# An MoE block on one core: tokens sorted by expert instead of by pair of experts, in tiles of 512 rows that are stored split in 16 bit and loaded transposed

## The chip, the cores and the metric

The kernel runs on one core of a Trainium2 chip. The metric is the device time of one execution, in microseconds (us). Five engines run side by side and meet through semaphores: TensorE (PE in the profile; PEld is its weight load), VectorE (DVE), ScalarE (ACT), GpSimd (POOL) and SyncE (SP). DMAs are issued from SP, ACT and POOL, and all of them run on the core's 16 DMA engines.

## The reference

The input x is 32 images of 128 channels and 32 x 32 pixels, f32. What is computed:

```
u  = layernorm over channels (x)
wt = (max(u) @ w2.T + b2) - (mean(u) @ w1.T + b1)    # 9 taps for each image and channel, softmax over the taps
x1 = x + u + depthwise_3x3(u, wt) + bias             # still image by image
t  = x1 as 32768 tokens of 128 features
q  = layernorm over features (t)
g  = q @ Wg + bg                                     # 8 logits; the two largest, softmax over those two
out = t + sum over the two chosen experts e of w_e * (gelu(q @ W1[e] + b1[e]) @ W2[e] + b2[e])   # 128 -> 512 -> 128
```

The products of the experts are made in f16 with the operands split in a high and a low half (high x high + low x high + high x low), at three times the work of one product.

## The kernel before, in words

There are three stages, one after the other. The order of the work is written out by hand for each engine; an engine does its list in that order and waits on semaphores.

**The conv stage** (`run_steps`) handles two images (16 blocks of 128 tokens) per step, in a pipeline of four sub-stages: layer norm and taps, convolution, turning into tokens with the statistics (`turn`, `token_std`, `keep`), and routing (`choose`, `ranks`, `place`, `weigh`). Each step of the loop thus does a part of four different pairs of images; there are 16 pairs. Routing finds for each token which of the 28 unordered pairs of experts it goes to, and its place in the list of this pair. GpSimd then writes the rows of a pair of images to DRAM with indirect DMAs, one for each block of 128 tokens, so 16 a step (line 439); the index of each row is computed on DVE. One row is 133 f32: the raw token, two weights, the token's number and two numbers with which ACT normalises it later. `rows` has two buffers: ACT's `keep` waits for the DMAs of the pair before the last (`rows_out`), and so does DVE's `place` for `idx`. After the last pair DVE makes a table of the tiles from the counts (lines 1087 to 1123), and SP and ACT write padding rows behind the end of each list (`pad`).

**The tile stage** runs over NT = 32768/256 + 28 = 156 tiles of 256 tokens, each with one pair of experts (`dstep` on PE, ACT and DVE, the loop of lines 442 to 454 on POOL). SP loads a tile's rows from DRAM into one of RING = 6 buffers as soon as the output of the tile six before has left (`y_out`). ACT normalises, PE transposes, ACT and DVE split the result in f16 halves. For each of the two experts PE does the up product (`up`: 12 matmuls of 256 columns), ACT the gelu, ACT or DVE the split of the hidden values, PE the down product (`down`: for each of 4 quarters of the hidden layer and 2 blocks of tokens one matmul of 256 columns against the weights' both halves and one of 128 columns; then the bias). DVE weighs and adds the two experts' results (`combine`), POOL adds the halves and the token itself (lines 447, 449) and writes the two blocks to their places in DRAM with an indirect DMA each (line 454).

**The final stage** loads each image's tokens (512 KB) from DRAM, PE turns them back to channels, DVE copies them from PSUM, and ACT issues the store of the image.

## Time and profile before

| | |
|---|---|
| median of 3 runs | 1804.54 us (1803.85 to 1805.2) |
| span of the profiled execution | 1798.2 us |
| own time of the profiled execution | not given apart; its span lies 6.3 us below the median of the runs |
| PE busy | 1536.5 us (85%) |
| DVE busy | 1396.4 us (78%) |
| ACT busy | 1202.0 us (67%) |
| POOL busy | 866.1 us (48%) |
| moved by DMA | 115.76 MB |

The span runs from the first to the last instruction. Busy is the time in which an engine had an instruction in it. Matmuls are pipelined, so that the duration of one is longer than the distance to the next; where a rate is needed, the distance from start to start is read. For POOL the busy time counts the instruction itself (for an indirect DMA the making of its descriptors), while the queue also spends time between two of them. Idle time of an engine is put down to whatever released it; "issue" is time in which nothing that the profile shows was waited for. The conv stage lasts from the start to about 669 us, the tile stage from there to 1705 us, the final stage to the end.

### The profile page before, as it was taken

The page shows a single profiled execution, that of the slowest core. Times are in us where ns is not written, and L with a number is a line of the kernel's source. Part 1 is how long each engine was busy: PE and PEld are TensorE (multiplying, and loading weights), DVE is VectorE, ACT ScalarE, POOL GpSimd, SP SyncE. Part 2 cuts the span into 40 slices and gives each one's busy share as a digit, 9 for nine tenths or more (in the row PEclk, how much of TensorE's full clock was granted, in tenths as well). Part 3 has the DMA queues.
Part 4 walks back from the last instruction along what each step waited for, and adds up shares of the span by engine and source line. Part 5 has one row for each costly group of instructions (what it writes and reads, how often), then busy time and mean ns, then how long its engine had stood idle before and what let it go on. Part 6 is the DMA issues. An engine that isn't in the chain of part 4 may idle for free.

```text
span 1798.2 us, 45758 instructions
## 1 busy us (share of the span) xinstructions
PE 1536.5 (85%) x12335; PEld 1186.0 (66%) x12336; DVE 1396.4 (78%) x2440; ACT 1202.0 (67%) x2949; POOL 866.1 (48%) x905
## 2 busy tenths in 40 slices
PE   5889999999999519999999999999999999999665
PEld 2445555555555307878888778878777788878555
DVE  0468888788788737888888888888888888888644
ACT  3466667767666308878777887788777887888400
POOL 1003455355355464555555555555555555555500
PEclk8899999999998659999999999999999999999965
DMA  3211121121121061111111111111111111110099
GB/s 120 59 35 56 54 72 59 59 70 60 61 58 49 31 146 30 39 39 36 42 42 37 36 38 39 39 40 35 41 42 37 40 38 42 42 37 22 22 374 359
DMA packets 90626, 115.76 MB, mean 64 GB/s; under 512 B 15286, under 2 KB 71794, under 8 KB 90583
## 3 DMA queue, kind: packets, MB, share of 16 engines
q1 hardware_dynamic: 65784, 62.29, 12.2%
q0 software_dynamic: 18176, 34.27, 5.5%
q10 hardware_dynamic: 6624, 18.69, 2.8%
q8 instruction: 20, 0.33, 0.1%
q14 instruction: 22, 0.18, 0.0%
HBM read 60.22 MB, written 58.61 MB: 66 GB/s over the span
## 4 chain that ended last, share of the span: by engine, by line
issue 31%; POOL 28%; PE 24%; ACT 7%; DMA 4%; DVE 4%; POOLq 1%; SPq 0%; ACTq 0%; DVEq 0%
POOL token_out L454 12%; POOL yt L449 9%; PE psV L731 8%; POOL yt L447 6%; DMA ye<-token_out 4%; PE psR L703 3%; PE psV L691 3%; ACT spent L531 2%; PE psA L682 2%; PE psT L716 2%; PE psR L747 2%; PE psG L718 1%; POOL rows_by_pair L439 1%; DVE x L963 1%; ACT sq L508 1%
## 5 line engine op out<-in xcount | busy, mean ns | idle before, releaser
L1138 DVE TENSOR_TENSOR gl<-g,gh 128x1024 f16<-128x1024 f32 x312 | 438.1, 1404 | 70.5 <-ACT gh L624 65.2
L439 POOL DMA_INDIRECT rows_by_pair<-rows,idx x256 | 265.0, 1035 | 393.3 <-issue 245.4
L454 POOL DMA_INDIRECT token_out<-yt,rt x312 | 323.1, 1036 | 184.6 <-POOL yt L449 133.5
L616 ACT ACTIVATE g<-psV,b1col 128x256 f32<-128x256 f32 x624 | 244.4, 474 | 143.6 <-PE psV L825 143.6
L616 ACT ACTIVATE g<-psT,b1col 128x256 f32<-128x256 f32 x624 | 244.4, 474 | 53.4 <-PE psT L825 53.4
L731 PE MATMUL psV<-lp,diag 128*128 128x512 f32 x512 | 254.2, 626 | 24.8 <-ACT cv L524 14.6
L823 PE MATMUL psV<-xh,wall 128*128 128x256 f16 x624 | 171.9, 275 | 94.6 <-DVE xl L1128 53.8
L447 POOL TENSOR_TENSOR yt<-ya 128x256 f32<-128x256 f32 x156 | 112.9, 724 | 247.0 <-DVE ya L1150 246.9
L841 PE MATMUL psG<-wall,gh 128*128 x1248 | 222.7, 273 | 1.7 <-DVE ya L1146 1.4
L841 PE MATMUL psR<-wall,gh 128*128 x1248 | 222.7, 273 | 0.7 <-DVE ya L1150 0.7
L842 PE MATMUL psG<-wall,gl 128*128 x1248 | 214.3, 219 | 0.0
L842 PE MATMUL psR<-wall,gl 128*128 x1248 | 214.3, 219 | 0.0
L963 DVE SCALAR_TENSOR_TENSOR x<-lp,taps,x 128x1024 f32<-128x1024 f32 x160 | 205.3, 1283 | 3.5
L1136 DVE CAST gh<-g 128x1024 f16<-128x1024 f32 x156 | 145.8, 934 | 70.2 <-ACT g L616 70.1
L731 PEld LDWEIGHTS psV<-lp,diag 128*128 128x128 f32 x512 | 97.0, 199 | 152.6 <-issue 104.2
L823 PE MATMUL psT<-xh,wall 128*128 128x256 f16 x624 | 171.9, 275 | 0.1
L824 PE MATMUL psV<-xl,wall 128*128 128x256 f16 x624 | 170.7, 274 | 0.0
L825 PE MATMUL psV<-xh,wall 128*128 128x256 f16 x624 | 170.7, 274 | 0.0
L824 PE MATMUL psT<-xl,wall 128*128 128x256 f16 x624 | 170.7, 274 | 0.0
L825 PE MATMUL psT<-xh,wall 128*128 128x256 f16 x624 | 170.6, 273 | 0.0
L624 ACT ACTIVATE gh<-g 128x1024 f16<-128x1024 f32 x156 | 164.9, 1057 | 5.0
L600 ACT ACTIVATE xn<-rt 128x128 f32<-128x128 f32 x312 | 139.9, 514 | 42.1 <-DMA rt<-rows_by_pair 42.1
(187 smaller groups left out, 3254.9 us busy)
## 6 DMA issues: line engine op xcount, KB each, us to landing
rt<-rows_by_pair SPq DMA_DIRECT2D x156, 133.0 KB, 2.1
xb<-in_x_dram SPq DMA_DIRECT2D x32, 512.0 KB, 3.5
ye<-token_out SPq DMA_DIRECT2D x32, 512.0 KB, 9.1
out_dram<-oe ACTq DMA_DIRECT2D x32, 512.0 KB, 5.8
token_out<-yt,rt POOLq DMA_INDIRECT x312, 2.3
rows_by_pair<-rows,idx POOLq DMA_INDIRECT x256, 2.4
stage<-in_L_ffn_W_dram SPq DMA_DIRECT2D x1, 2048.0 KB, 12.3
rows_by_pair<-pad_rows SPq DMA_DIRECT2D x15, 133.0 KB, 5.2
```

The lines of the kernel that those rows point to most:

```text
L439: gp.indirect_dma_start(rows_dram, bass.IndirectOffsetOnAxis(ap=idx[p][:, b:b + 1].bitcast(U32), axis=0), rows[p][:, b, :], None).then_inc ...
L447: gp.tensor_tensor(yt[r][:, :, :], ya[r][:, :, 0:D], ya[r][:, :, D:2 * D], ALU.add).then_inc(ysum_done, 1)
L454: gp.indirect_dma_start(y_dram, bass.IndirectOffsetOnAxis(ap=rt[r][:, b, ID:ID + 1].bitcast(U32), axis=0), yt[r][:, b, :], None, bounds_ch ...
L616: last = sc_.activation(g[side][:, s * T:(s + 1) * T], hbank[side][:, s * T:(s + 1) * T], ACT.Gelu, bias=b1col[:, bass.ds(e * HS + s, 1)], ...
L731: ins = te.matmul(psConv.rearrange("p (h w) -> p h w", w=WW), diag[k][:, m, :], lp[j][:, y:y + HH // 2, dx:dx + WW], start=(m == 0), stop= ...
L823: te.matmul(out_, high, xh[q][:, :], start=True, stop=False)
L824: te.matmul(out_, high, xl[q][:, :], start=False, stop=False)
L825: last = te.matmul(out_, wall[:, bass.ds(w + (O_1L + s * P), P)], xh[q][:, :], start=False, stop=True)
L841: te.matmul(bank[:, 2 * b * D:2 * (b + 1) * D], gh[side][:, lhs], both, start=(s == 0 and b == 0), stop=False, skip_group_check=True)
L842: te.matmul(bank[:, 2 * b * D:(2 * b + 1) * D], gl[side][:, lhs], high, start=False, stop=False, skip_group_check=True)
L963: ins = v.scalar_tensor_tensor(out=img(x1[j]), in0=lp[j][:, dy:dy + HH, dx:dx + WW], scalar=taps[st_.slot(stage)][:, DVE_TAPS[m], k:k + 1] ...
L1138: v.tensor_tensor(gl[side][:, :], g[side][:, :], gh[side][:, :], ALU.subtract).then_inc(lo_done, 1)
```

## The change

Each token is written twice, once into the list of each of its two experts. There are 8 lists and NT = 2 x 32768/512 + 8 = 136 tiles of 512 rows, each with one expert.

- In the conv stage ACT normalises the token (`normalise`) and makes its high f16 half (`high`), DVE the low half (`low`). A row is 130 f32 wide: 128 f16 high, 128 f16 low, the number of the output row and the weight. A second buffer, `twin`, gets the same halves by a DMA from SP (`copy_rows`) and has its own number and weight. POOL writes 8 blocks of `rows`, the same 8 of `twin`, then the other image's: 32 indirect DMAs a step. DVE's routing works on 8 columns a block and not on 28, and finds two places for each token.
- The sum of the convolution, x1, is stored to DRAM by SP image by image (`store_x1`), and DVE's `add_image` waits for the store of two pairs before.
- In the tile stage SP loads the halves of 512 rows with a transposing DMA into `xt`, and number and weight with a second DMA into `meta` (pieces of 8 bytes). The ring has 4 buffers and not 6. ACT's normalising, PE's transposes and the splitting of the input are gone. PE's `up` is 4 x 3 matmuls of 512 columns, `down` 4 x 4 x 3 matmuls of 128 columns, and 4 of 128 columns for the bias. ACT does four gelus of 512 columns and casts two of the quarters, DVE casts the other two, makes the four low halves and weighs the result in one operation. POOL only issues the indirect DMAs, 4 a tile. Each token's two results stay apart, in an output of 65536 rows.
- SP reads x1 of the first 16 images back in the tile stage, behind the first four tiles' loads.
- In the final stage SP loads both results of each image's tokens (1 MB) and x1 of the other 16 images, PE turns both, and DVE adds them and x1 in two operations.

The diff, cut to its core (removed functions stand above in the kernel before):

```diff
-    NPAIR = E * (E - 1) // 2
-    T = 2 * P
+    T = 4 * P
     TB = T // P
-    CAP = NTOK + 2 * T
-    NT = NTOK // T + NPAIR
+    CAP = NTOK + T
+    NT = 2 * NTOK // T + E
-    RW = D + 5
-    W_LO, W_HI, ID, NMR, RSTD = range(D, D + 5)
+    XW = D // 2
+    ID, W = 2 * XW, 2 * XW + 1
+    RW = 2 * XW + 2
-    RING = 6
-    rows_dram = nc.dram_tensor("rows_by_pair", [NREG * CAP + T, RW], F32).ap()
-    y_dram = nc.dram_tensor("token_out", [NTOK, D], F32).ap()
+    RING = 4
+    rows_dram = nc.dram_tensor("rows_by_expert", [E * CAP + T, RW], F32).ap()
+    y_dram = nc.dram_tensor("choice_out", [2 * NTOK, D], F32).ap()
+    x1_dram = nc.dram_tensor("conv_out", [NIMG, C, PIX], F32).ap()
...
+            def copy_rows(st_, stage, k):
+                p, blks = st_.slot(stage), slice(k * NBLK, (k + 1) * NBLK)
+                sp.wait_ge(low_ready, st_.count(stage, 2, k + 1))
+                sp.dma_start(twin[p][:, blks, 0:2 * XW], rows[p][:, blks, 0:2 * XW]).then_inc(twin_in[2 * p + k], 16)
...
             def load_rows(first, r):
-                sp.dma_start(rt[r][:, :, :], rows_dram[bass.ds(first, T), :].rearrange("(p b) f -> p b f", b=TB)).then_inc(row_in[r], 16)
+                src = rows_dram[bass.ds(first, T), :]
+                sp.dma_start_transpose(xt[r][:, :, :], src[:, 0:2 * XW].bitcast(F16)).then_inc(row_in[r], 16)
+                sp.dma_start(meta[r][:, :, :], src[:, ID:RW].rearrange("(b p) f -> p b f", p=P)).then_inc(row_in[r], 16)
             for r in range(RING):
-                first = sp.value_load(tab[0:1, TW * r:TW * r + 1], min_val=0, max_val=NREG * CAP)
+                first = sp.value_load(tab[0:1, TW * r:TW * r + 1], min_val=0, max_val=E * CAP)
                 load_rows(first, r)
...
+                load_x1(j, j)
             with sp.Fori(1, NT // RING, 1) as t:
                 for r in range(RING):
...
+                    first = sp.value_load(tab[0:1, bass.ds((RING * t + r) * TW, 1)], min_val=0, max_val=E * CAP)
                     sp.wait_ge(y_out[r], 16 * TB * t)
                     load_rows(first, r)
...
+            y_v = y_dram.rearrange("(k n b p) d -> n p k b d", k=2, b=NBLK, p=P)
+            def load_e(n, j):
+                for k in range(2):
+                    src = y_v[n] if isinstance(n, int) else y_v[bass.ds(n, 1)].rearrange("a p k b d -> (a p) k b d")
+                    sp.dma_start(ye[j][:, k, :, :], src[:, k, :, :]).then_inc(ye_in[j], 16)
             for j in range(4):
...
+                load_e(j, j)
+            for n in range(4, NIMG):
+                sp.wait_ge(yT_ready, n - 3)
+                load_e(n, n % 4)
+                if n - 4 + NX < NIMG:
+                    sp.wait_ge(half_ready, n - 3)
+                    load_x1(n - 4 + NX, (n - 4) % NX)
...
-                    pool.wait_ge(kept, images)
-                    for b in range(NB2):
-                        gp.indirect_dma_start(rows_dram, bass.IndirectOffsetOnAxis(ap=idx[p][:, b:b + 1].bitcast(U32), axis=0),
-                                              rows[p][:, b, :], None).then_inc(rows_out[2 * p + b // NBLK], 16)
+                    pool.wait_ge(low_ready, images)
+                    for k in range(2):
+                        for c, src in enumerate((rows[p], twin[p])):
+                            if c == 1:
+                                pool.wait_ge(s_const, 3)
+                                pool.wait_ge(twin_in[2 * p + k], copies)
+                            for b in range(k * NBLK, (k + 1) * NBLK):
+                                gp.indirect_dma_start(rows_dram, bass.IndirectOffsetOnAxis(ap=idx[p][:, c, b:b + 1].bitcast(U32), axis=0),
+                                                      src[:, b, :], None).then_inc(rows_out[2 * p + k], 16)
+            pool.reg_mov(tiles, 2)
             with pool.Fori(0, NT // RING, 1) as t:
                 for r in range(RING):
-                    pool.wait_ge(ya_done, 2 * (RING * t + r) + 4)
-                    gp.tensor_tensor(yt[r][:, :, :], ya[r][:, :, 0:D], ya[r][:, :, D:2 * D], ALU.add).then_inc(ysum_done, 1)
-                    pool.wait_ge(ysum_done, RING * t + r + 1)
-                    gp.tensor_tensor(yt[r][:, :, :], yt[r][:, :, :], rt[r][:, :, 0:D], ALU.add).then_inc(yt_done, 1)
                     pool.reg_alu(tiles, tiles, 1, ALU.add)
                     pool.wait_ge(s_const, 3)
                     pool.wait_ge(yt_done, tiles)
                     for b in range(TB):
-                        gp.indirect_dma_start(y_dram, bass.IndirectOffsetOnAxis(ap=rt[r][:, b, ID:ID + 1].bitcast(U32), axis=0),
-                                              yt[r][:, b, :], None, bounds_check=NTOK - 1, oob_is_err=False).then_inc(y_out[r], 16)
+                        gp.indirect_dma_start(y_dram, bass.IndirectOffsetOnAxis(ap=meta[r][:, b, 0:1].bitcast(U32), axis=0),
+                                              yt[r][:, b, :], None, bounds_check=2 * NTOK - 1, oob_is_err=False).then_inc(y_out[r], 16)
...
+            def normalise(st_, k):
                 p = st_.slot(3)
+                act.wait_ge(nmr_ready, st_.count(3, 2, k + 1))
+                for b in range(NBLK):
+                    at = slice(k * NBLK + b, k * NBLK + b + 1)
+                    last = sc_.activation(nrm[k][:, b, :], psT[:, b * P:(b + 1) * P], ACT.Identity, bias=nmr[p][:, at], scale=rstd[p][:, at])
+                last.then_inc(normed, 1)
+            def high(st_, k):
+                p = st_.slot(3)
+                act.wait_ge(normed, st_.count(3, 2, k + 1))
                 if not st_.fixed or st_.turns(3) > 0:
...
+                    act.wait_ge(rows_out[2 * p + k], 32 * NBLK * st_.turns(3))
+                sc_.activation(x_high(rows[p], k), nrm[k][:, :, :], ACT.Copy).then_inc(xh_ready, 1)
...
+            def gelu(j, q):
+                at = TW * j + T_EXP
                 e = act.value_load(tab[0:1, at:at + 1] if isinstance(j, int) else tab[0:1, bass.ds(at, 1)], min_val=0, max_val=E - 1)
...
+                def cast(s):
+                    act.wait_ge(g_done, HS * j + s + 1)
+                    if s == 0:
+                        act.wait_ge(y_ready, j + 1)
+                    sc_.activation(gh[q][s][:, :], g[q][s][:, :], ACT.Copy).then_inc(hi_act, 1)
                 for s in range(HS):
...
+                    act.wait_ge(h_ready, HS * j + s + 1)
+                    act.wait_ge(lo_done, HS * j + s + 1)
+                    sc_.activation(g[q][s][:, :], hbank[s], ACT.Gelu, bias=b1col[:, bass.ds(e * HS + s, 1)], scale=1.0 / WSCALE).then_inc(g_done, 1)
+                    if s - 1 in ACT_CAST:
+                        cast(s - 1)
...
+            def up(j, r, s, t):
+                w = weights(r)
+                if s == 0:
+                    pe.wait_ge(row_in[r], 32 * (t + 1))
+                if not isinstance(j, int) or j >= 1:
+                    pe.wait_ge(g_done, HS * j + s + 1 - HS)
+                high = wall[:, bass.ds(w + (O_1H + s * P), P)]
+                te.matmul(hbank[s], high, xt[r][:, 0, :], start=True, stop=False)
+                te.matmul(hbank[s], high, xt[r][:, 1, :], start=False, stop=False)
+                te.matmul(hbank[s], wall[:, bass.ds(w + (O_1L + s * P), P)], xt[r][:, 0, :], start=False, stop=True).then_inc(h_ready, 1)
+            def down(j, r, s):
+                w, q = weights(r), r % 2
+                pe.wait_ge(lo_done, HS * (j + 2) + s + 1)
+                if s in ACT_CAST:
+                    pe.wait_ge(hi_act, len(ACT_CAST) * j + ACT_CAST.index(s) + 1)
+                if s == 0:
+                    pe.wait_ge(yt_done, j + 1)
+                bank = ybank[q]
+                high = wall[:, bass.ds(w + (O_2 + 2 * s * D), D)]
+                low = wall[:, bass.ds(w + (O_2 + (2 * s + 1) * D), D)]
                 for b in range(TB):
...
+                    lhs, at = slice(b * P, (b + 1) * P), bank[:, b * D:(b + 1) * D]
+                    te.matmul(at, gh[q][s][:, lhs], high, start=(s == 0 and b == 0), stop=False, skip_group_check=True)
+                    te.matmul(at, gh[q][s][:, lhs], low, start=False, stop=False, skip_group_check=True)
+                    te.matmul(at, gl[q][s][:, lhs], high, start=False, stop=False, skip_group_check=True)
+                if s == HS - 1:
+                    bias = wall[:, bass.ds(w + O_B2, D)]
+                    for b in range(TB):
+                        last = te.matmul(bank[:, b * D:(b + 1) * D], bias_sel[:, :], bias, start=False, stop=(b == TB - 1), skip_group_check=True)
+                    last.then_inc(y_ready, 1)
+            pe.sem_inc(y_ready, 2)
+            expert(0, 0)
+            expert(1, 1)
+            for s in range(HS):
+                up(0, 0, s, 0)
+            def dstep(j, r, t):
+                more = not isinstance(j, int)
                 for s in range(HS):
...
+                    if more or j + 1 < NT:
+                        up(j + 1, (r + 1) % RING, s, t + (r + 1) // RING)
+                    if s == 1 and (more or j + 2 < NT):
+                        expert(j + 2, (r + 2) % RING)
+                    down(j, r, s)
...
+            def low(st_, stage, k):
+                p = st_.slot(stage)
+                dve.wait_ge(xh_ready, st_.count(stage, 2, k + 1))
+                v.tensor_tensor(x_low(rows[p], k), nrm[k][:, :, :], x_high(rows[p], k), ALU.subtract).then_inc(low_ready, 1)
...
+            def parts(j, q):
+                for s in range(HS):
+                    if s in ACT_CAST:
+                        dve.wait_ge(hi_act, len(ACT_CAST) * j + ACT_CAST.index(s) + 1)
                     else:
...
+                        dve.wait_ge(g_done, HS * j + s + 1)
+                        if s == HS - 2:
+                            dve.wait_ge(y_ready, j + 1)
+                        v.tensor_copy(gh[q][s][:, :], g[q][s][:, :]).then_inc(hi_dve, 1)
+                        dve.wait_ge(hi_dve, (HS - len(ACT_CAST)) * j + s - len(ACT_CAST) + 1)
+                    v.tensor_tensor(gl[q][s][:, :], g[q][s][:, :], gh[q][s][:, :], ALU.subtract).then_inc(lo_done, 1)
+            def combine(j, r):
+                q = r % 2
+                dve.wait_ge(y_ready, j + 3)
+                v.tensor_tensor(yt[r][:, :, :], ybank[q].rearrange("p (b d) -> p b d", d=D), meta[r][:, :, 1:2].broadcast_to([P, TB, D]), ALU.mult).then_inc(yt_done, 1)
...
+                a, b = ((psA, psV), (psT, psH))[n % 2]
+                dve.wait_ge(yT_ready, n + 1)
+                dve.wait_ge(x1_in[n % NX], 16 * (n // NX + 1))
+                v.tensor_tensor(mid[n % 2][:, :], a[:, :], x1c[n % NX][:, :], ALU.add).then_inc(half_ready, 1)
+                dve.wait_ge(half_ready, n + 1)
+                dve.wait_ge(o_out[n % 4], 16 + 16 * (n // 4))
+                v.tensor_tensor(oe[n % 4][:, :], b[:, :], mid[n % 2][:, :], ALU.add).then_inc(o_ready, 1)
```

## Rows read from the trace of the kernel before

**Rows 1.** The page, part 4: the chain that ended last, by engine.

```profile
issue 31%; POOL 28%; PE 24%; ACT 7%; DMA 4%; DVE 4%; POOLq 1%; SPq 0%; ACTq 0%; DVEq 0%
```

**Rows 2.** Windows: us, busy us per engine (PE, PEld, DVE, ACT, POOL), clock, DMA share, GB/s.

```profile
180.00:360.00 180.00, 173.26 (x794) 101.74 (x793) 148.29 (x361) 123.80 (x355) 83.07 (x81) 0.97 0.19 61
...
1260.00:1620.00 360.00, 325.92 (x3422) 288.15 (x3420) 311.81 (x442) 288.15 (x664) 209.31 (x221) 1.00 0.13 40
...
1720.00:1798.00 78.00, 46.54 (x216) 38.88 (x216) 32.95 (x27) 0.00 (x0) 0.00 (x0) 0.61 1.05 369
```

**Rows 3.** Line 439: ns min/median/max, first and last start.

```profile
L439 POOL DMA_INDIRECT rows_by_pair<-rows,idx x256: 963/968/1927, 155.8 to 665.2; - x128
```

**Rows 4.** Groups by line, 180 to 540 us: busy us, mean ns, idle before.

```profile
L439 POOL DMA_INDIRECT rows_by_pair<-rows,idx x167 | 173.4, 1039 | 189.8 <-issue 189.8
```

**Rows 5.** Timeline at the end of the conv stage and the start of the tile stage.

```profile
665.20 0.97 POOL L439 DMA_INDIRECT rows_by_pair<-rows,idx  x1 [0.30 <-issue]
...
669.15 28.94 SPq L369 DMA_DIRECT2D rt<-rows_by_pair  x7
```

**Rows 6.** Groups by line, 900 to 1500 us (92 tiles).

```profile
L1138 DVE TENSOR_TENSOR gl<-g,gh 128x1024 f16<-128x1024 f32 x184 | 258.8, 1407 | 41.1 <-ACT gh L624 37.9
...
L454 POOL DMA_INDIRECT token_out<-yt,rt x184 | 190.1, 1033 | 110.1 <-POOL yt L449 78.7 <-issue 31.4
...
L616 ACT ACTIVATE g<-psV,b1col 128x256 f32<-128x256 f32 x368 | 144.1, 474 | 87.0 <-PE psV L825 87.0
...
L624 ACT ACTIVATE gh<-g 128x1024 f16<-128x1024 f32 x92 | 97.2, 1057 | 2.9
...
L1136 DVE CAST gh<-g 128x1024 f16<-128x1024 f32 x92 | 86.2, 937 | 39.4 <-ACT g L616 39.4
...
L1146 DVE TENSOR_SCALAR ya<-psG,rt 128x256 f32<-128x256 f32 x184 | 79.2, 469 | 0.0
...
L842 PEld LDWEIGHTS psR<-wall,gl 128*128 128x128 f16 x736 | 72.0, 98 | 0.3
```

**Rows 7.** Timeline of PE within one tile, 1203 to 1210 us.

```profile
1202.85 0.28 PE L823 MATMUL psV<-xh,wall 128*128 128x256 f16 x1 [0.49 <-ACT g L616]
...
1204.06 0.27 PE L825 MATMUL psV<-xh,wall 128*128 128x256 f16 x1
...
1205.70 0.28 PE L845 MATMUL psG<-wall,bias_sel 128*128 x2
...
1205.83 0.28 PE L823 MATMUL psT<-xh,wall 128*128 128x256 f16 x1
```

**Rows 8.** Timeline of PE in a step of the conv stage.

```profile
589.24 1.81 PE L747 MATMUL psR<-pairs,ones_b 128*128 128x448 bf16 x16
...
590.89 1.54 PE L731 MATMUL psV<-lp,diag 128*128 128x512 f32 x3
```

**Rows 9.** Timeline of a tile's last indirect DMA and SP's next load.

```profile
1203.34 0.97 POOL L454 DMA_INDIRECT token_out<-yt,rt  x1 [0.30 <-issue]
...
1205.76 0.34 SPq L369 DMA_DIRECT2D rt<-rows_by_pair  x1
```

**Rows 10.** SP's own waits, the whole span.

```profile
SPq L369 <- DMA token_out<-yt,rt: 806.2, 150, 21.7
```

**Rows 11.** The page, part 6: DMA issues, KB each, median us to landing.

```profile
rt<-rows_by_pair SPq DMA_DIRECT2D x156, 133.0 KB, 2.1
...
xb<-in_x_dram SPq DMA_DIRECT2D x32, 512.0 KB, 3.5
...
ye<-token_out SPq DMA_DIRECT2D x32, 512.0 KB, 9.1
...
token_out<-yt,rt POOLq DMA_INDIRECT x312, 2.3
```

**Rows 12.** Timeline at the change to the final stage.

```profile
1705.00 79.69 SPq L385 DMA_DIRECT2D ye<-token_out  x32
...
1712.20 83.31 ACTq L653 DMA_DIRECT2D out_dram<-oe  x32
```

More of the change, by code:

```diff
@@ new lines, in conv_moe_block @@
+        m1, m2, s1, s2, gap, e2, den = (sb(n, [P, NB2]) for n in ("m1", "m2", "s1", "s2", "gap", "e2", "den"))
+        onehot = sb("onehot", [P, NB2, E], BF16)
+        both_h = sb("both_choices", [P, 2, NB2, E])
+        pos = sb("pos", [P, NB2, E])
+        sel2 = sb("sel2", [P, 2, NB2, E])
+        idf = sb("idf", [P, 2, NB2])
+        base = sb("base", [P, E])
+        idx = [sb(f"idx{p}", [P, 2, NB2], I32) for p in range(2)]
+        cnt, tiles_f, tend, zeros_e, ge, sel = (sb(n, [P, E]) for n in ("cnt", "tiles_f", "tend", "zeros_e", "ge", "sel"))
@@ L425, in _ @@
             images = pool.alloc_register("images")
+            copies = pool.alloc_register("copies")
             tiles = pool.alloc_register("tiles")
-            for reg in (routed, images, tiles):
+            for reg in (routed, images, copies):
                 pool.reg_mov(reg, 0)
             with pool.Fori(0, NU // 2, 1) as t:
+                pool.reg_alu(copies, copies, 16, ALU.add)
                 for p in range(2):
@@ L529, in token_std @@
                 act.wait_ge(stat_ready, n)
+                if not st_.fixed or st_.count(3, 2, k) > 1:
+                    act.wait_ge(low_ready, st_.count(3, 2, k - 1))
                 for b in range(NBLK):
-                    last = sc_.activation(spent[:, b * P:(b + 1) * P], psT[:, b * P:(b + 1) * P], ACT.Square, bias=negm[st_.slot(3)][:, k * NBLK + b:k * NBLK + b + 1],
+                    last = sc_.activation(nrm[k][:, b, :], psT[:, b * P:(b + 1) * P], ACT.Square, bias=negm[st_.slot(3)][:, k * NBLK + b:k * NBLK + b + 1],
                                           accum_out=ssq[:, b:b + 1])
@@ L586, in _ @@
             act.wait_ge(tab_ready, 1)
-            for k in range(NPAIR // 2 + 1, NPAIR + 1):
+            for k in range(E // 2, E + 1):
                 pad(act, k)
             act.wait_ge(tab_in, 16)
-            def normalise(j, r, t):
-                q = r % 2
-                act.wait_ge(row_in[r], 16 * (t + 1))
-                if not isinstance(j, int) or j >= 2:
-                    act.wait_ge(xT_ready, j - 1)
-                for b in range(TB):
-                    last = sc_.activation(xn[q][:, b, :], rt[r][:, b, 0:D], ACT.Identity, bias=rt[r][:, b, NMR:NMR + 1], scale=rt[r][:, b, RSTD:RSTD + 1])
-                last.then_inc(xn_done, 1)
@@ L828, in down @@
-            def down(j, side, o):
-                w = weights(o, side)
-                pe.wait_ge(lo_done, 2 * j + side + 1)
-                pe.wait_ge((hi0_done, hi1_done)[side], j + 1)
-                pe.wait_ge(ya_done, 2 * j + side + 1)
-                bank = ybank[side]
-                for s in range(HS):
-                    both = wall[:, bass.ds(w + (O_2 + 2 * s * D), 2 * D)]
-                    high = wall[:, bass.ds(w + (O_2 + 2 * s * D), D)]
-                    for b in range(TB):
-                        lhs = slice(s * T + b * P, s * T + (b + 1) * P)
-                        te.matmul(bank[:, 2 * b * D:2 * (b + 1) * D], gh[side][:, lhs], both, start=(s == 0 and b == 0), stop=False, skip_group_check=True)
-                        te.matmul(bank[:, 2 * b * D:(2 * b + 1) * D], gl[side][:, lhs], high, start=False, stop=False, skip_group_check=True)
-                bias = wall[:, bass.ds(w + O_B2, D)]
-                for b in range(TB):
-                    last = te.matmul(bank[:, 2 * b * D:(2 * b + 1) * D], bias_sel[:, :], bias, start=False, stop=(b == TB - 1), skip_group_check=True)
-                last.then_inc(y_ready, 1)
@@ L1009, in choose @@
-                last.then_inc(pairs_ready, 1)
+                v.tensor_tensor(onehot[:, :, :], both_h[:, 0, :, :], both_h[:, 1, :, :], ALU.add).then_inc(onehot_ready, 1)
             def weigh(st_):
                 link = c4.link
-                r_ = rows[st_.slot(4)]
+                a_, b_ = rows[st_.slot(4)], twin[st_.slot(4)]
                 dve.wait_ge(e2_ready, st_.count(4, 1, 1))
                 link(v.tensor_scalar(den[:, :], e2[:, :], WSCALE, WSCALE, ALU.mult, ALU.add))
-                link(v.reciprocal(wa[:, :], den[:, :]))
@@ L1066, in step @@
                     norm(st_, 1)
+                if st_.on(3):
+                    low(st_, 3, 0)
                 if st_.on(4):
@@ new lines, in _ @@
+                combine(j, r)
+            for n in range(NIMG):
+                a, b = ((psA, psV), (psT, psH))[n % 2]
[5 more added lines that the diff above has]
+                v.tensor_tensor(oe[n % 4][:, :], b[:, :], mid[n % 2][:, :], ALU.add).then_inc(o_ready, 1)
```

449 lines of the change are left out of this document (159 added, 290 removed).

## Prediction, made before the change was run

> **What bounds the kernel now.** The chain of waits is read first: most of it is POOL and "issue" [rows 1], so a lightly busy engine is often the one waited for. The windows then show three stages with different limits [rows 2]. In the conv stage PE is busy for 173.3 of 180 us, DVE for 148.3. A step takes 34.5 us (167 indirect DMAs in 360 us are 10.4 groups of 16 [rows 4]). POOL needs 16 x (1.04 + 0.30) = 21.4 us of it; the 0.30 is the gap between two of its DMAs, which the timeline shows without any releaser [rows 4, 5]. In the tile stage 92 tiles take 600 us [rows 6], 6.52 us each: PE and DVE are both near 88% busy and hand work to each other. The final stage is bound by DMA: share 1.05 at 369 GB/s [rows 2].
>
> The span of 1798.2 us splits so: 155.8 until POOL's first row DMA [rows 3], 513.4 to SP's first tile load at 669.15 [rows 5], 1035.8 to the first load of the final stage at 1705.00 [rows 12], 93.2 to the end. The profiled execution's span lies 6.3 under the median of the runs; I add these 6.3 at the end.
>
> **Conv stage.** What goes from DVE (28 columns against 8 in the routing) and what comes (one low half per image, 1.2 to 1.4 us by the like operation of 1024 columns [rows 6]) nearly cancel. ACT gives up one copy of 1.0 us per image and gets 8 normalising operations (some 0.4 each, an estimate from half of a 256-column one's 0.47 plus its start-up [rows 6]) and one cast of 1.06 [rows 6]: some 6.5 us more per step, on an engine busy 123.8 of 180 us, so 24 becomes 30 us a step. Neither reaches 34.5. SP's new stores of x1 and its `twin` copies add 1.5 MB a step, at 61 GB/s and a DMA share of 0.19 [rows 2] hidden.
>
> POOL is another matter. It has 32 indirect DMAs a step instead of 16. At 0.97 + 0.30 unloaded [rows 3, 5] that is 40.6 us, at the mean of 1.04 + 0.30 [rows 4] 42.9; with a little for the waits on `twin_in` I take 42.8. That is over 34.5: POOL becomes the bound, and its work is serial on one queue. Do the waits behind it lengthen the step further? ACT's `high` for image 0 waits for the first half of the DMAs of the pair before the last (21.4 + 2.4 us after POOL turned to it), then DVE's `low`, `place` and `weigh` need some 6 us until the next pair is released: 30 us, under 42.8. So POOL has always work waiting. The first group starts at 155.8 + 4 (the fuller early steps), 16 groups take 685, so the last ends at 845; table and padding are made beside POOL's last group. From the last DMA's end to SP's load are 3.0 us (665.20 + 0.97 to 669.15 [rows 5]). SP's first tile load comes at 848 instead of 669: **+179**. Bounds: 40.6 a step gives 812, 44 a step 868; if POOL were hidden, 669.
>
> **Tile stage, the engines' sums per tile.** PE: a matmul of 256 columns comes every 0.110 us (11 distances from 1202.85 to 1204.06 [rows 7]), so 12 of 512 take 2.6. The 52 of 128 columns each load weights of their own. The nearest row are the two of the bias, 0.13 for both [rows 7], and the 16 of the conv stage that load 16 times and take 1.65 us in all, which is their 3808 columns at 2.4 GHz (1.59) and little more, though six of them are 168 columns or shorter [rows 8]. I take 0.056 each: 2.9. A weight load's own duration, 98 ns [rows 6], is the other end: 5.1. PE: 5.5, at most 7.7. DVE: four low halves at half of 1.41, two casts at half of 0.94, one weighing of 512 columns at about 0.8: 4.5. ACT: four gelus of 512 columns at 0.65 (between 0.47 for 256 and 1.06 for a cast of 1024 [rows 6]) and two casts at 0.6: 3.8. POOL: 4 x (1.03 + 0.30) and some 0.35 for the registers and waits of a tile: 5.65 (unloaded: 4 x 1.27 + 0.3 = 5.4). Its two additions are gone. So PE and POOL are level at 5.5 to 5.65, where 6.52 x 156 = 1017 us would become 5.65 x 136 = 768.
>
> The TensorE page of the Trainium skill ("TensorE: Matmul & The Clock Gate", Back-to-back issue gap) has a sustained 81 ns for 128 columns where each matmul has a weight load, against 56 ns for matmuls alone; by that an estimate for `down` is 4.2 us, and the sum would be some 60 us more.
>
> **Tile stage, the ring.** The load of a tile waits until the output of the tile four before has left; before it was six, and SP was already always waiting for that, 806 us in 150 waits [rows 10], with the loads landing early enough. Now follow one turn. A load lands and `up` of tile j+4 may begin; PE's order puts the quarters of tile j+3's `down` between those of that `up`, one slot of 5.5 us. DVE's `combine` of j+3 stands behind all splitting of j+4: after `up`'s third quarter come gelu 0.65, cast 0.6, low 0.7, cast 0.45, low 0.7, cast 0.45, low 0.7, combine 0.8, and some 0.7 for hand-overs, 5.75, of which 2.2 lie within the slot: 3.55. POOL 5.65. The last DMA lands 2.3 us after its start [rows 11], 1.3 after its end, and SP's next load follows at once (1203.34 to 1205.76 are 2.42 [rows 9]): 1.5 with the hand-over. Then the load itself, X, and `up` of tile j+7 may begin. Three tiles in 5.5 + 3.55 + 5.65 + 1.5 + X = 16.2 + X. This beats 5.65 a tile as soon as X is over 0.8 us.
>
> X is a transposing DMA of 256 KB and behind it a DMA of 512 pieces of 8 bytes. No row shows a transposing DMA. From below: 133 KB land in 2.1, 512 KB in 3.5 [rows 11], so 2.6 for the size, plus 0.34 of issue for the second [rows 9]: 3. From above: 9.1, the landing of 512 KB in pieces of 512 bytes with four in the queue [rows 11]. I take 4, nearer to the idle queue of the tile stage (share 0.13 [rows 2]). That gives 20.2/3 = 6.7 us a tile, 136 x 6.7 = **911**, with the ends 6.4 (870) and 8.4 (1147). The fill and the tail were 1035.8 - 1017 = 19, I take 20 (16 loads of x1, 8.4 MB, go out once and are hidden but for the first turn). So 931 against 1035.8: **-105**.
>
> The page "DMA: Bandwidth & Descriptors" of the Trainium skill (Latency and other measured facts) gives 261 GB/s for a transposing DMA with a non-contiguous middle dimension, which would be 1.0 us for the 256 KB; by that X would be near 3 and a tile 6.4. No row here can show it.
>
> **Final stage.** Now 32 MB are moved in 93.2 us: 16.8 in, 16.8 out, at 369 GB/s with about 2.3 us left over at the ends [rows 2, 12]. Then 33.6 MB of results, 8.4 of x1, 16.8 out: 58.7 MB, at 369 GB/s 159 us, with 7 us for the first load's way (1705.00 to 1712.20 [rows 12]) 166. PE (16 transposes, 2 x 1.5 us an image) and DVE (2.5) stay under the 5.0 us of DMA per image. **+73**. Bounds: 150 to 180.
>
> **Sum.** 848 + 931 + 166 = 1945, + 6.3 = 1951. Against 1804.5: +146, which is +179 - 105 + 73.
>
> **Rivals.**
> 1. *The transposing load is slow* (X of 6 and more). For it: two DMAs, tiny pieces, the wait is on the path. Against: the DMA engines are nearly idle. At X = 8: 8.07 x 136 = 1097, total 2137; at X = 6 2046. Chance 0.20.
> 2. *Weight loads pace `down`.* For it: rows 7 and 8 never show more than three full matmuls of 128 columns in a row, and here are 48; a load takes 98 ns by itself. Against: in both rows loads overlap, 0.13 us for two. At 98 ns a tile is PE's 7.7: 1047, total 848 + 1067 + 166 + 6 = 2087; halfway between, 77 ns, it is 6.6 a tile for PE and the ring decides again. Chance 0.08. (The skill's page named above stands between the two.)
> 3. *Faster: the ring never closes.* The place is SP's wait on `y_out`; if `combine` and the load follow so soon that a tile costs what PE does, 5.5, the tile stage is 748 + 20. With POOL unloaded in both stages (no additions of its own, 1.27 an indirect DMA: conv stage to 828) the total is 828 + 768 + 166 + 6 = 1768. It decides below 5.7 us a tile (828 + 20 + 166 + 6 + 136 x 5.74 = 1801). For it: every engine's own sum is under 5.7. Against: the turn above needs X below 1, and X has two landings. Chance 0.11.
> 4. *POOL's added DMAs in the conv stage are hidden*: 34.5 a step stays, the total is 1951 - 133 to 179, 1772 to 1818. The change would then not cost what its count says. Only other work on POOL's queue could hide it, and there is none: chance 0.04, half of it within 0.2%.
>
> The forecast (6.2 to 7.1 us a tile, POOL bound in the conv stage) has 0.57. This kernel's measurement tells 0.2% from no change. Faster: 0.12 (rival 3 and a part of 4). Same: 0.02. Slower: 0.86. The range takes in X from about 2 to 7 with the bounds of the two other stages: 1830 to 2090.
>
> **What would show it.** Right: POOL's indirect DMAs of the conv stage back to back with 0.30 between them, no long idle time before a group, 41 to 44 us a step, the first tile load near 848. In the tile stage PE's idle time before `up` put down to the DMA of `xt` or `meta`, some 1.2 us a tile; SP waiting for the output DMAs in nearly every tile; 6.7 us a tile. In the final stage a DMA share of 1 for some 160 us. Wrong: an idle POOL in the conv stage; PE without waits for rows (then the ring was not closed); matmuls of `down` spaced by 80 ns; a load that lands after more than 6 us.

## The result, and the profile after

The changed kernel takes 2034.1 us (median of 4 runs, 2029.4 to 2038.3) against 1804.4: a ratio of 1.128, 95% interval 1.125 to 1.130. Slower was forecast, 1951 us, with a range of 1830 to 2090. The profiled execution took 2037.7 us, its span 2035.9.

The stages come from the first and last start of the lines that begin and end them (ns min/median/max, then the two starts):

```profile
L488 POOL DMA_INDIRECT rows_by_expert<-rows,idx x256: 963/968/2019, 165.1 to 841.5; - x128
L488 POOL DMA_INDIRECT rows_by_expert<-twin,idx x256: 963/967/1949, 176.9 to 851.7; - x128
  issue: 155.8, 511
...
L397 SPq DMA_TRANSPOSE xt<-rows_by_expert x136: 1246/1261/3052, 855.1 to 1831.6; - x136
...
L424 SPq DMA_DIRECT2D ye<-choice_out x64: 371/1660/3569, 1856.8 to 2019.0; - x64
```

| | before | forecast | after |
|---|---|---|---|
| first row DMA of POOL | 155.8 | 160 | 165.1 |
| a step of the conv stage | 34.5 | 42.8 | 43.0 |
| first tile load | 669.2 | 848 | 855.1 |
| tile stage, to the first load of the final stage | 1035.8 | 931 | 1001.7 |
| final stage | 93.2 | 166 | 179.1 |

A step is (851.7 + 1.3 - 165.1)/16. So of +237.7 in the spans, +185.9 is the conv stage, -34.1 the tile stage, +85.9 the final stage.

The windows of the changed kernel, columns as in [rows 2], answer to that group:

```profile
360.00:540.00 180.00, 152.43 (x626) 87.78 (x627) 115.60 (x231) 118.82 (x333) 139.27 (x134) 0.85 0.37 122
...
1200.00:1700.00 500.00, 418.61 (x4473) 300.63 (x4471) 285.26 (x490) 264.89 (x420) 294.43 (x280) 0.93 0.34 73
...
1900.00:1950.00 50.00, 25.31 (x133) 22.84 (x131) 20.77 (x18) 0.00 (x0) 0.00 (x0) 0.76 1.10 347
```

In the conv stage no engine looks like a bound by its busy time: POOL is busy for 139.3 of 180 us. But 134 DMAs with a gap of 0.30 each are 139.3 + 40.6 = 180: the queue has no other idle time. The line "issue: 155.8, 511" above says the same of the whole stage, 511 gaps of 0.305 us and no wait but the first. In the tile stage, where [rows 2] had 91% of PE and 87% of DVE, all engines are under 84%. The waits of the whole span name the reason (us in total, times, longest):

```profile
POOL choice_out L500 <- DVE yt L1134: 272.6, 60, 20.9
...
PE psA L839 <- DMA meta<-rows_by_expert: 242.9, 56, 79.5
...
SPq L397 <- DMA choice_out<-yt,meta: 554.1, 127, 14.5
```

SP waited for the output DMAs before too [rows 10], but only the first tile's load was waited for then. Now PE waits in nearly every turn (79.5 of the 242.9 are the wait for the first tile). The ring closes when the load of a tile has waited for the output of the tile four before, and PE has nothing left to do until it lands. One closing, in the chain of waits (start, us, what):

```profile
1213.10 2.26 DMA choice_out<-yt,meta
1215.47 1.26 SPq L397
1216.95 2.67 DMA meta<-rows_by_expert
1219.61 0.24 issue
1219.86 0.39 PE psA L839
```

From the load's start to `up` are 4.39 us. The load of three tiles later starts at 1235.18; I call this stretch a turn. These are the windows of five turns in a row:

```profile
1215.47:1235.18 19.71, 15.90 (x187) 11.50 (x185) 11.99 (x21) 10.51 (x17) 11.45 (x13) 1.00 0.37 80
1235.18:1255.25 20.07, 16.75 (x194) 12.00 (x192) 12.10 (x22) 11.24 (x19) 12.33 (x13) 1.00 0.36 79
1255.25:1280.31 25.06, 21.30 (x216) 15.09 (x213) 14.04 (x25) 12.96 (x21) 13.98 (x13) 0.86 0.30 63
1280.31:1302.99 22.68, 18.28 (x180) 13.10 (x181) 10.54 (x19) 10.67 (x17) 12.50 (x12) 0.85 0.32 64
1302.99:1324.63 21.64, 18.29 (x198) 13.21 (x196) 12.26 (x22) 11.42 (x19) 12.90 (x13) 0.92 0.34 73
```

Two turns take 19.7 and 20.1 us at a granted clock of 1.00; the other three are longer, at 0.85 to 0.92. The third in four parts, before PE's wait, the wait, and two parts of what PE does after it:

```profile
1255.25:1257.03 1.78, 1.78 (x24) 1.26 (x21) 1.16 (x3) 1.60 (x3) 1.48 (x2) 1.00 0.21 42
1257.03:1260.01 2.98, 0.00 (x1) 0.00 (x1) 2.52 (x5) 0.00 (x0) 2.37 (x3) 0.85 0.65 130
1260.01:1265.93 5.92, 5.92 (x32) 3.74 (x33) 0.53 (x1) 1.89 (x3) 4.35 (x5) 0.50 0.42 89
1265.93:1280.31 14.38, 13.60 (x161) 10.09 (x159) 9.84 (x18) 9.47 (x15) 5.79 (x5) 1.00 0.19 41
```

The clock is at 1.00 until the wait, falls within it, and is at 0.50, which is 1.2 GHz, for the 5.9 us after it. PE's timeline has the same two levels:

```profile
1260.01 0.60 PE L839 MATMUL psA<-xt,wall 128*128 128x512 f16 x1 [2.98 <-DMA meta<-rows_by_expert]
...
1262.55 0.63 PE L839 MATMUL psA<-xt,wall 128*128 128x512 f16 x1
1263.40 0.63 PE L841 MATMUL psA<-xt,wall 128*128 128x512 f16 x1
...
1269.69 0.38 PE L839 MATMUL psA<-xt,wall 128*128 128x512 f16 x1
1270.12 0.38 PE L841 MATMUL psA<-xt,wall 128*128 128x512 f16 x1
```

Lines 839 and 841 are two matmuls of 512 columns apart: 0.85 us at 1262.55, 0.43 at 1269.69. The whole stage's mean is (1001.7 - 20)/136 = 7.22 us a tile, 21.7 a turn. There are 42 turns of three tiles that lie between two such waits. In 12 the granted clock is 1.00, and 11 of these take 19.6 to 20.3 us, 19.8 in the mean (one takes 21.6). In 15 it is 0.92: 21.5 to 22.0 us. In 13 it is 0.85: 22.7 to 23.0. The other two are the first (27.2 us at 0.76) and the one above (25.1 at 0.86).

### The profile page after: what moved, and what is told of

Its sections match the earlier page's. It is cut to its first block, busy times and chain, and to the rows that moved or that the text cites. A ratio compares the mean times of both kernels' runs of the same rounds, so it can differ in the third digit from the quotient of the medians.

```text
span 2035.9 us, 39735 instructions
## 1 busy us (share of the span) xinstructions
PE 1516.3 (74%) x11623; PEld 1023.5 (50%) x11624; DVE 1091.8 (54%) x1954; ACT 993.5 (49%) x2149; POOL 1115.0 (55%) x1083
## 4 chain that ended last, share of the span: by engine, by line
PE 25%; issue 20%; DMA 17%; POOL 15%; ACT 10%; DVE 6%; SPq 5%; POOLq 0%; ACTq 0%; DVEq 0%
POOL rows_by_expert L488 10%; PE psV L760 6%; DMA meta<-rows_by_expert 6%; POOL choice_out L500 6%; DMA ye<-choice_out 5%; DMA choice_out<-yt,meta 5%; PE psV L720 3%; SPq L397 3%; ACT gh L662 2%; ACT nrm L593 2%; ACT nrm L579 2%; PE psA L839 2%; DVE gh L1126 2%; PE psT L745 2%; DMA rows_by_expert<-twin,idx 1%
## 5 line engine op out<-in xcount | busy, mean ns | idle before, releaser
L500 POOL DMA_INDIRECT choice_out<-yt,meta x544 | 575.6, 1058 | 427.4 <-DVE yt L1134 272.6
L1128 DVE TENSOR_TENSOR gl<-g,gh 128x512 f16<-128x512 f32 x544 | 377.4, 694 | 505.6 <-ACT gh L662 496.3
L856 PE MATMUL psT<-wall,gh 128*128 x2176 | 417.2, 227 | 0.5 <-DVE gl L1128 0.4
L857 PE MATMUL psT<-wall,gh 128*128 x2176 | 416.5, 227 | 0.0
L858 PE MATMUL psT<-wall,gl 128*128 x2176 | 416.2, 227 | 0.0
L488 POOL DMA_INDIRECT rows_by_expert<-rows,idx x256 | 270.1, 1055 | 234.5 <-DVE twin L1034 156.8
L760 PE MATMUL psV<-lp,diag 128*128 128x512 f32 x512 | 286.3, 694 | 58.7 <-ACT diag L562 41.3
L488 POOL DMA_INDIRECT rows_by_expert<-twin,idx x256 | 261.7, 1022 | 78.0 <-issue 78.0
L839 PE MATMUL psA<-xt,wall 128*128 128x512 f16 x272 | 118.2, 435 | 243.3 <-DMA meta<-rows_by_expert 242.9
L856 PEld LDWEIGHTS psT<-wall,gh 128*128 128x128 f16 x2176 | 222.4, 102 | 80.4 <-issue 29.9
L857 PEld LDWEIGHTS psT<-wall,gh 128*128 128x128 f16 x2176 | 222.4, 102 | 65.8 <-issue 12.7
L858 PEld LDWEIGHTS psT<-wall,gl 128*128 128x128 f16 x2176 | 222.5, 102 | 0.0
L667 ACT ACTIVATE g<-psV,b1col 128x512 f32<-128x512 f32 x272 | 187.0, 687 | 39.9 <-PE psV L841 11.7
L839 PEld LDWEIGHTS psA<-xt,wall 128*128 x272 | 28.4, 105 | 253.8 <-issue 253.5
L840 PE MATMUL psA<-xt,wall 128*128 128x512 f16 x272 | 116.2, 427 | 0.0
L841 PE MATMUL psA<-xt,wall 128*128 128x512 f16 x272 | 115.3, 424 | 0.0
```

The lines of the kernel that those rows point to most:

```text
L488: gp.indirect_dma_start(rows_dram, bass.IndirectOffsetOnAxis(ap=idx[p][:, c, b:b + 1].bitcast(U32), axis=0), src[:, b, :], None).then_inc( ...
L500: gp.indirect_dma_start(y_dram, bass.IndirectOffsetOnAxis(ap=meta[r][:, b, 0:1].bitcast(U32), axis=0), yt[r][:, b, :], None, bounds_check= ...
L667: sc_.activation(g[q][s][:, :], hbank[s], ACT.Gelu, bias=b1col[:, bass.ds(e * HS + s, 1)], scale=1.0 / WSCALE).then_inc(g_done, 1)
L760: ins = te.matmul(psConv.rearrange("p (h w) -> p h w", w=WW), diag[k][:, m, :], lp[j][:, y:y + HH // 2, dx:dx + WW], start=(m == 0), stop= ...
L839: te.matmul(hbank[s], high, xt[r][:, 0, :], start=True, stop=False)
L856: te.matmul(at, gh[q][s][:, lhs], high, start=(s == 0 and b == 0), stop=False, skip_group_check=True)
```

## Experiments

**More buffers.** In `ring8` only the number of ring buffers changes, timed in 3 rounds.

```diff
-    RING = 4
+    RING = 8
```

> The changed kernel with 8 ring buffers instead of 4 in the tile stage, nothing else. Theory (the ring closes: SP's load of tile j+4 waits for the output of tile j, three tiles take 16.2 us + the load's 4.4 + what the cold TensorE adds after each wait): with 8 buffers a turn spreads over seven tiles, 21 to 22 us / 7 is 3 us, so nothing waits for it and a tile costs what PE or POOL need, 5.5 to 5.7 us. Tile stage 136 x 5.65 + 20 = 790 us against 1002, PE's granted clock 1.00 in its middle against 0.93, no PE wait for the DMA of meta; total about 1825. Rival (loads are slow because the DMA engines or the transposing path are short of throughput, whatever the number of buffers): the tile stage stays above 950 us and the waits for the DMA of meta stay.

```profile
L397 SPq DMA_TRANSPOSE xt<-rows_by_expert x136: 1245/1264/4689, 857.1 to 1585.0; - x136
L424 SPq DMA_DIRECT2D ye<-choice_out x64: 372/1687/3743, 1628.1 to 1790.0; - x64
...
1000.00:1500.00 500.00, 500.00 (x5829) 371.19 (x5827) 370.65 (x638) 344.38 (x547) 385.40 (x365) 1.00 0.43 95
```

1808.3 us, a ratio to the kernel before of 1.002 (1.000 to 1.004). The tile stage takes 1628.1 - 857.1 = 771.0 us. PE is busy in all of the 500 us, at a clock of 1.00, with no wait for a load; 364 low halves, 91 tiles, are 5.49 us a tile. The DMA engines carry more (share 0.43 against 0.34), so they had room. The theory holds and the rival of slow loads falls: 231 us of the change's time are the ring. PE is not alone at its limit now. The groups by line, 1000 to 1500 us, show POOL full as well, 386.4 us in its DMAs and 114.9 in the gaps between them:

```profile
L500 POOL DMA_INDIRECT choice_out<-yt,meta x365 | 386.4, 1059 | 114.9 <-issue 114.9
```

**Four buffers, an earlier load.** `early_xt` keeps 4 buffers. SP loads the halves once `up` of the tile four before is done, and number and weight after that tile's output as before, with a semaphore of their own (`meta_in`) for which DVE's `combine` waits.

```diff
-                    sp.wait_ge(y_out[r], 16 * TB * t)
-                    load_rows(first, r)
+                    sp.wait_ge(h_ready, HS * (RING * t + r - RING + 1))
+                    load_x(first, r)
...
+                        sp.wait_ge(y_out[q], 16 * TB * t if r > 0 else 16 * TB * (t - 1))
+                        load_m(first, q)
```

> The changed kernel with its ring of 4, but the halves of tile j+4 are loaded as soon as PE's up product of tile j is done; only number and weight wait for the output of tile j, and only DVE's combine waits for them. Theory (what costs in the tile stage is that the load waits for the output's DMAs at the end of a long chain, not the number of buffers and not the transfer itself): PE no longer waits for a load, its clock stays at 1.00, a tile takes 5.5 us as with 8 buffers, the tile stage 765 to 790 us, total 1800 to 1830. Rival (4 buffers are too few in any case, because loads take long): the tile stage stays above 900.

```profile
1000.00:1500.00 500.00, 500.00 (x5830) 371.19 (x5827) 367.85 (x638) 344.35 (x547) 387.96 (x363) 1.00 0.44 95
...
L439 SPq DMA_DIRECT2D ye<-choice_out x64: 363/1664/3490, 1637.5 to 1799.4; - x64
```

One run, 1819.9 us, and the same full 500 us of PE. The first load starts at 852.8, so the tile stage is 784.7 us, within what was expected and 14 more than in `ring8`; the middle is the same, so the 14 lie at the ends. So 4 buffers suffice: what costs is that the whole load waits for the output.

**The parts of the load.** `plain_load` replaces the transposing DMA by a plain one of the same bytes, which makes other products.

```diff
-                sp.dma_start_transpose(xt[r][:, :, :], src[:, 0:2 * XW].bitcast(F16)).then_inc(row_in[r], 16)
+                sp.dma_start(xt[r][:, :, :].rearrange("p a t -> p (a t)").rearrange("p (b f) -> p b f", b=TB),
+                             src[:, 0:2 * XW].bitcast(F16).rearrange("(p b) f -> p b f", b=TB)).then_inc(row_in[r], 16)
```

> The changed kernel, but the halves are loaded with a plain DMA of the same bytes, not a transposing one (so the products are of other numbers). Theory (it is the ring's length that costs, of which the transposing DMA is a part): the load's 4.4 us from issue to up fall by the transposing DMA's longer issue (1.26 against 0.34 to 0.45 us) and what its transfer takes more, to 3.3 us or so; a turn of three tiles gets 1 to 1.5 us shorter, the tile stage 136/3 x 1.2 = 50 to 70 us shorter, 930 to 950 us. Rival (the transposing DMA is the slow part, as X = 6 or more in the prediction had it): the tile stage falls to 850 or less.

```profile
1211.90 0.55 SPq L397 DMA_DIRECT2D xt<-rows_by_expert  x1
1212.65 0.47 SPq L398 DMA_DIRECT2D meta<-rows_by_expert  x1
...
1215.60 0.39 PE L839 MATMUL psA<-xt,wall 128*128 128x512 f16 x1 [3.05 <-DMA meta<-rows_by_expert]
```

One run, 2020.3 us. From load to `up` 3.70 us instead of 4.39 in the closing shown: what is saved is the issue on SP (0.55 against 1.26). The tile stage, 852.6 to 1839.8, is 987.2 us, 14.5 less. That misses the 50 to 70 that were expected, and it is less than the 0.7 x 45 turns = 31 that the load itself gained. The tile stage of the changed kernel, with no edit in it, took 1018.2 us in `no_x1_back` below, so single runs of it differ by more than that, and the 14.5 us themselves are not shown. The rival of a slow transposing path (850 or less) falls clearly.

`meta_first` issues the small DMA first.

> The changed kernel with the two DMAs of a load issued in the other order: number and weight first, then the halves. Theory (of the 4.4 us from a load's start to up, 1.26 + 0.2 + 0.43 are issue on SP and the landing of the small pieces is the last 2.7): the transposing DMA now starts 0.6 us later and lands last; if its own landing takes 2.5 us from its issue's end as well, up starts 4.4 us after the load's start again and the tile stage stays within 20 us of 1002. Rival (the 512 pieces of 8 bytes are what takes long, the transposing DMA lands sooner): the load gets 0.5 to 1 us shorter and the tile stage 25 to 45 us.

```profile
1222.62 0.39 SPq L397 DMA_DIRECT2D meta<-rows_by_expert  x1
1223.15 1.26 SPq L398 DMA_TRANSPOSE xt<-rows_by_expert  x1
...
1226.91 0.61 PE L839 MATMUL psA<-xt,wall 128*128 128x512 f16 x1 [3.67 <-DMA xt<-rows_by_expert]
```

One run, 2036.4 us, tile stage 999.2 (1855.8 - 856.6), load to `up` 4.29. The order does not matter: the transposing DMA lands 2.5 us after its issue ends (1224.41 to 1226.91, PE's start included), as the 4 KB of `meta` did.

**POOL's count in the conv stage.** `no_twin` counts and writes only each token's first choice, 16 row DMAs a step; the final stage reads the first results twice. Half of its tiles are padding, so only its conv stage is read.

```diff
-                        for c, src in enumerate((rows[p], twin[p])):
-                            if c == 1:
+                        for c, src in enumerate((rows[p],)):
+                            if c == 0:
...
-                v.tensor_tensor(onehot[:, :, :], both_h[:, 0, :, :], both_h[:, 1, :, :], ALU.add).then_inc(onehot_ready, 1)
+                v.tensor_copy(onehot[:, :, :], both_h[:, 0, :, :]).then_inc(onehot_ready, 1)
```

> The changed kernel, but only each token's first choice is counted and written: 16 row DMAs per step of the conv stage instead of 32, everything else in the conv stage kept (also the copy of the rows by SP). The final stage reads the first result twice. About half of the tiles are padding then, so only the conv stage is read. Theory (POOL's queue paces the conv stage): a step falls from 43.0 us to what PE, DVE and ACT need, 34 to 36 us, and POOL shows idle time before each group; the first tile load comes at 720 to 745 us instead of 855. Rival (ACT's and DVE's added work and the stores pace it): a step stays at 41 to 43, the first load comes after 820.

```profile
161.85 1.16 POOL L488 DMA_INDIRECT rows_by_expert<-rows,idx  x1 [153.58 <-DVE twin L1034]
201.41 0.97 POOL L488 DMA_INDIRECT rows_by_expert<-rows,idx  x1 [17.24 <-issue]
239.65 0.97 POOL L488 DMA_INDIRECT rows_by_expert<-rows,idx  x1 [15.80 <-issue]
...
660.42 0.97 POOL L488 DMA_INDIRECT rows_by_expert<-rows,idx  x1 [13.75 <-issue]
```

These are the first DMAs of a step's group. From the second group to the one at 660.42 each comes after 14 to 19 us of an idle queue. The first tile load comes at 733.0, so POOL's second 16 DMAs cost 122 us of the 186. But a step is 38.35 us ((660.42 - 161.85)/13), not 34 to 36: the conv stage's other additions cost 3.9 us a step, which the full change hides under POOL. Which of them (ACT's eight normalising operations, or waits between PE, ACT and DVE that they lengthen) was not tried. One trace of it is PE's granted clock, 0.89 and 0.92 here in the windows 180 to 360 and 360 to 540 us, against 0.97 before [rows 2].

**The bytes of the final stage.** `no_x1_back` leaves out the second 16 reads of x1 and adds the first images' twice.

```diff
-                if n - 4 + NX < NIMG:
-                    sp.wait_ge(half_ready, n - 3)
-                    load_x1(n - 4 + NX, (n - 4) % NX)
...
-                dve.wait_ge(x1_in[n % NX], 16 * (n // NX + 1))
+                dve.wait_ge(x1_in[n % NX], 16)
```

> The changed kernel, but x1 of images 16 to 31 is not read back in the final stage (the first 16 images' is added twice), 8.4 MB less. Theory (the final stage is bound by the bytes that DMA moves, 58.7 MB in 179 us): 50.3 MB at the same rate, 345 GB/s in its middle, is 24 us less, 155 us. Rival (bound by the chain of ye's loads over PE's transposes and DVE's two additions with four buffers): within 5 us of 179.

```profile
L424 SPq DMA_DIRECT2D ye<-choice_out x64: 372/1740/4227, 1878.0 to 2019.3; - x64
```

The span ends at 2035.6, so the final stage takes 157.6 us instead of 179.1: 21.5 for 8.4 MB, at 390 GB/s, near the 24 of the theory. With these reads go SP's waits for DVE between them, 10.7 us in the changed kernel's waits, so bytes and waits are not fully apart; but 10.7 is half of what was gained. The total, 2037.4, is no less, because this run's tile stage, whose code is the changed kernel's, took 16.5 us more. The whole tile stage's window in the changed kernel, and then in this run:

```profile
855.08:1856.84 1001.76, 821.78 (x8704) 588.87 (x8704) 552.98 (x952) 515.94 (x817) 575.60 (x544) 0.91 0.35 78
...
859.82:1877.98 1018.16, 837.11 (x8704) 600.33 (x8704) 551.39 (x952) 515.34 (x817) 576.92 (x544) 0.89 0.34 77
```

Of the busy times only PE's differs by more than 2 us: it is 15.3 us longer, at a lower granted clock.

**One part of the change alone, on the kernel before.** `pairs_down128` keeps pairs, tiles of 256 tokens and everything else, and makes only the down product in matmuls of 128 columns; so DVE weighs half as many columns and POOL has one addition a tile instead of two. 3 rounds.

```diff
-                        te.matmul(bank[:, 2 * b * D:2 * (b + 1) * D], gh[side][:, lhs], both, start=(s == 0 and b == 0), stop=False, skip_group_check=True)
-                        te.matmul(bank[:, 2 * b * D:(2 * b + 1) * D], gl[side][:, lhs], high, start=False, stop=False, skip_group_check=True)
+                        te.matmul(at, gh[side][:, lhs], high, start=(s == 0 and b == 0), stop=False, skip_group_check=True)
+                        te.matmul(at, gh[side][:, lhs], low_, start=False, stop=False, skip_group_check=True)
+                        te.matmul(at, gl[side][:, lhs], high, start=False, stop=False, skip_group_check=True)
```

> One part of the change alone, on the kernel before: pairs of experts, tiles of 256 tokens, 156 of them, all as before, but the down product in matmuls of 128 columns that add high and low parts in PSUM. PE's columns stay the same; DVE weighs 512 columns a tile instead of 1024, POOL loses one of its two additions. Theory (matmuls of 128 columns with a weight load each cost their columns, 0.055 us, and DVE is the second bound of the tile stage before): PE's sum stays at 5.9 us a tile, DVE's falls from 5.65 to about 4.8, a tile takes 6.1 to 6.3 instead of 6.52, the total is 1740 to 1775. Rival (weight loads pace small matmuls, 77 to 81 ns each): down takes 48 x 0.025 = 1.2 us more a tile, 7.1 or more, the total is above 1890.

```profile
900.00:1500.00 600.00, 562.89 (x7364) 508.40 (x7362) 439.57 (x662) 493.17 (x1135) 304.17 (x284) 1.00 0.13 40
...
L369 SPq DMA_DIRECT2D rt<-rows_by_pair x156: 331/333/387, 670.7 to 1644.9; - x156
...
L385 SPq DMA_DIRECT2D ye<-token_out x32: 372/566/4775, 1678.5 to 1755.6; - x32
```

1775.6 us, a ratio of 0.985 (0.981 to 0.988): this beats both kernels, the one before by 1.5%. 95 casts of `gh` in the 600 us are 6.32 us a tile against 6.52, the tile stage 1007.8 against 1035.8. PE's load rises to 94%, DVE's falls to 73%. Tile and total are just above what was expected (6.1 to 6.3, 1740 to 1775): PE's own sum is 5.93 us a tile (562.9/95), and the hand-overs keep the other 0.4, most of it waits for ACT's `xh` and gelu.

## Why the prediction was right, and where its terms were off

The signs and mechanisms of all three stages were right, and every stage came out longer than forecast: +230 us against +146, so the total lies in the upper half of the range.

**Conv stage: right, +179 against +186.** Thirty-two serial row DMAs pace the step, 43.0 us against 42.8 forecast. The 7 us that are missing are the start (165.1, not 160) and 3 us over the 16 steps, less 0.6 at SP's first load. ACT's and DVE's busy times do stay under 34.5 us a step (28.4 and 27.6, from the window of 360 to 540 us), but it was wrong to conclude that without POOL a step would: `no_twin` shows 38.35. I had added up busy times and no waits. Nor are the stores of x1 and the `twin` copies 1.5 MB a step: four DMAs of 512 KB are 2.1. Both cost nothing, as POOL needs more.

**Tile stage, the engines' sums: right.** PE's 5.5 a tile is 5.49 in `ring8`, and POOL is level with it, as forecast. The matmuls of 128 columns, in the changed kernel's PE timeline, three from one line 856 to the next:

```profile
1402.42 0.22 PE L856 MATMUL psT<-wall,gh 128*128 x1
...
1402.59 0.22 PE L856 MATMUL psT<-wall,gh 128*128 x1
```

0.17 us for three, 0.057 each, in a run of 12 such matmuls with their weight loads. So rival 2 did not happen, and `pairs_down128` gets faster with such matmuls. The 81 ns that the Trainium skill ("TensorE: Matmul & The Clock Gate", Back-to-back issue gap) has for a matmul of 128 columns with a weight load are not what these traces show.

**Tile stage, the ring: the mechanism right, its size too small.** PE's waits for the load, without the first tile's, are (242.9 - 79.5)/136 = 1.2 us a tile, as the prediction gave for its sign. The turn of three tiles was to take 16.2 + X, X = 4, so 20.2. X measures 4.39 in the turn shown (median of all the waits 4.28), and a turn at full clock takes 19.8 in the mean, so the 16.2 was some 0.7 too much. That is POOL's term, read from its timeline in the turn from 1215.47 to 1235.18:

```profile
1228.94 0.98 POOL L500 DMA_INDIRECT choice_out<-yt,meta  x1 [4.03 <-DVE yt L1134]
...
1232.80 0.98 POOL L500 DMA_INDIRECT choice_out<-yt,meta  x1 [0.30 <-issue]
```

Four DMAs take 4.84 us from the first start to the last end, and not 5.65: the gap behind the fourth and the registers of a tile do not lie on this path. The rest fits: 9.08 us from `up` (1219.86) to the first of them against 5.5 + 3.55, and 1.40 from the last end to the load against 1.5. Too much here and too little in X nearly cancel, by luck. How X is made up was wrong as well: I had 2.6 us of it for the size, but in this ring 256 KB and 4 KB both land some 2.5 us after their issue (`meta_first` and the changed kernel), and 1.26 us of X is the transposing DMA's issue.

What failed is the step from the turn to the stage: I priced PE's slot at 2.4 GHz throughout. The clock falls in some of the waits that the ring makes, and the next slot then starts at 1.2 GHz, as in the turn taken apart above. That is so in 30 of the 42 turns, and they take 22.5 us in the mean against 19.8. The mean of all is 21.7, so 1.5 us more than 20.2, 45 times: 68 of the 70.7 us by which the tile stage missed (some 6 of them in the first turn, 27 us long, which runs beside the 16 loads of x1). Where PE never waits (the middle of `ring8` and `early_xt`) the clock stands at 1.00. Why the clock falls in some waits and not in others of the same length stays open. That it makes the turns longer rests on the two levels within one turn, on the lengths of the turns, which go by the granted clock, and on `no_x1_back`, whose unchanged tile stage had less of the clock and took longer; a run that keeps the wait and holds the clock up was not made.

**Final stage: right, 13 us short.** The rate in its middle is 347 GB/s, not 369, 10 us on 58.7 MB; and the first store is issued 12.3 us after the first load instead of 7, since two results have to land and be turned first. Together that is 15, 2 more than are missing. That mostly bytes bound it, `no_x1_back` and a DMA share of 1.10 show.

**The rivals.** A slow transposing load did not happen: X was 4.4, and with a plain DMA it is still 3.7. The ring that never closes (rival 3) is `ring8`: its tile stage of 771 us is that rival's 768, but the conv and final stages hold the total at 1808. Hidden row DMAs (rival 4) are ruled out by the 511 gaps without a wait.

**Outside the stages** I had added 6.3 us; this execution has 1.8 beyond its span. The 6.3 compared one execution's span with the median of others.

## What to carry to other kernels

Count the instructions of a queue that issues one by one, times duration and gap, per step: POOL at 77% busy was full in the conv stage. When a buffer's reload waits for the end of the chain that empties it, write out one whole turn and divide by the tiles it spans, before believing any engine's sum; then see which of the buffer's parts are free sooner, as the halves were after `up`. A wait on PE can cost more than its length: turns in which the clock fell took some 2.5 us more than the others.

## What the runs showed of the hardware that was not expected

- An indirect DMA of 128 rows holds POOL's queue for 0.97 to 0.98 us and a gap of 0.30, whether the row has 532, 520 or 512 bytes (lines 439 before, 488 and 500 after).
- A transposing DMA of 256 KB is issued by SP in 1.26 us, the plain one of the same bytes in 0.55, and lands some 2.5 us after that, as a DMA of 4 KB does.
- A wait of 3 us on PE was followed by matmuls at 1.2 GHz for about 6 us (1260.01 to 1266), while waits as long or longer in other turns (3.68 us before 1219.86) were not.
